# ScalarE hands the diagonal blocks of a head attention to transfers, and some vector work changes engine

## What is computed

```python
def _L0_xattn_ref(inputs, context, Wq, Wk, Wv, Wcq, Wck, Wcv, gamma, beta, W1, b1):
    ...
    a = _attention(inputs, inputs, inputs, Wq, Wk, Wv, causal=True) + inputs
    h = _layer_norm(a, gamma, beta)
    c = _attention(h, context, context, Wcq, Wck, Wcv, causal=False) + h
    h = _layer_norm(c, gamma, beta)
    f = jax.nn.relu(jnp.einsum('bse,ed->bsd', h, W1) + b1)
    out = _layer_norm(f + h, gamma, beta)
    return jax.nn.relu(out)

def _L0_attn_ref(x, W_attn, W_proj):
    ...
    att = jnp.einsum('bhqd,bhkd->bhqk', q, k) * (1.0 / math.sqrt(hd))
    causal = jnp.tril(jnp.ones((T, T), dtype=bool))
    att = jnp.where(causal, att, -jnp.inf)
    att = jax.nn.softmax(att, axis=-1)
    att = att * decay_weight_matrix(T)
    y = jnp.einsum('bhqk,bhkd->bhqd', att, v)
    y = y.transpose(0, 2, 1, 3).reshape(B, T, HEAD_QKV)
    return y @ W_proj

x = x + _L0_xattn_ref(_layernorm(x, axis=-1), ctx_1024, ...)
x = x + _L0_attn_ref(_layernorm(x, axis=-1), L0_attn_W_attn, L0_attn_W_proj)
x = x + _L0_ffn_ref(_layernorm(x, axis=-1), ...)
```

## Time and profile before

| | |
|---|---|
| median of 3 runs | 1451.5 us (1449.05 to 1451.91) |
| span of the profiled execution | 1452.8 us |
| PE busy | 1365.6 us |
| DVE busy | 1128.1 us |
| ACT busy | 601.9 us |
| POOL busy | 526.1 us |

### The profile page before, as it was taken

How to read it: one execution, slowest core, us unless ns; L and a number is a source line. 1 busy time by engine, 2 the same in 40 slices (tenths; PEclk the granted TensorE clock), 3 DMA queues, 4 the chain that set the end, 5 groups by cost and what they waited for, 6 DMA issues and landing times.

```text
span 1452.8 us, 33270 instructions
## 1 busy us (share of the span) xinstructions
PE 1365.6 (94%) x13860; PEld 851.7 (59%) x13861; DVE 1128.1 (78%) x2335; ACT 601.9 (41%) x1147; POOL 526.1 (36%) x545
## 2 busy tenths in 40 slices
PE   7679999999999999999999999999999999998888
PEld 3355566666656666665665656666665666655443
DVE  6787777777787877778778877777778877777776
ACT  2544444443444444343434444444444444443222
POOL 0133333433444333443443333343443433343222
PEclk9899999999999999999999999999999999999899
DMA  9732444433333444433333344443333344434440
GB/s 349 259 131 74 146 146 146 144 123 105 133 112 115 146 146 146 146 137 101 122 130 105 139 146 146 146 142 114 111 138 105 123 146 146 147 134 161 149 161 30
DMA packets 38662, 201.41 MB, mean 139 GB/s; under 512 B 5096, under 2 KB 5992, under 8 KB 28400
## 3 DMA queue, kind: packets, MB, share of 16 engines
q1 hardware_dynamic: 37648, 198.93, 38.3%
q10 hardware_dynamic: 864, 0.36, 0.1%
HBM read 182.24 MB, written 17.04 MB: 137 GB/s over the span
## 4 chain that ended last, share of the span: by engine, by line
PE 70%; DVE 19%; POOL 4%; ACT 4%; issue 3%; DMA 0%; DVEq 0%; POOLq 0%; ACTq 0%; SPq 0%
PE ps_a L1716 11%; PE ps_a L1739 8%; PE ps_t L1739 7%; PE ps_t L1703 6%; PE ps_a L1725 6%; PE ps_a L1751 4%; PE ps_a L1783 4%; POOL rstd L636 4%; PE ps_t L1716 3%; PE ps_v L1716 3%; DVE stats L1178 3%; DVE arena L1309 3%; PE ps_t L1826 2%; PE ps_t L1775 2%; PE ps_t L1751 2%
## 5 line engine op out<-in xcount | busy, mean ns | idle before, releaser
L645 POOL TENSOR_TENSOR act_l<-act_t,act_h 128x512 f16<-128x512 f32 (+1 forms) x176 | 199.5, 1134 | 351.4 <-ACT act_t L789 199.4
L636 POOL TENSOR_TENSOR rstd<-var,mhalf 128x1 f32<-128x1 f32 x224 | 181.8, 812 | 333.7 <-DVE var L1180 328.9
L781 ACT ACTIVATE act_h<-ps_t,scale 128x512 f16<-128x512 f32 (+1 forms) x110 | 70.8, 644 | 206.2 <-PE ps_t L1703 206.2
L645 POOL TENSOR_TENSOR last_slot<-last_slot 128x512 f16<-128x512 f32 x80 | 90.0, 1125 | 156.7 <-ACT last_slot L789 90.8
L1739 PE MATMUL ps_a<-act_h,arena 128*128 128x128 f16 x1408 | 87.6, 221 | 17.3 <-ACT act_h L781 17.3
L1739 PEld LDWEIGHTS ps_a<-act_h,arena 128*128 128x128 f16 x1408 | 81.9, 99 | 28.3 <-ACT act_h L781 21.3
L789 ACT ACTIVATE act_t<-ps_t,scale 128x512 f32<-128x512 f32 (+1 forms) x110 | 70.3, 639 | 49.1 <-PE ps_t L1703 49.1
L1739 PE MATMUL ps_t<-act_h,arena 128*128 128x128 f16 x1408 | 87.0, 221 | 3.3 <-ACT act_h L781 3.3
L1716 PE MATMUL ps_a<-arena,act_h 128*128 128x512 f16 x352 | 83.6, 380 | 1.9 <-ACT act_h L781 1.9
L1309 DVE TENSOR_SCALAR arena<-ps_a,unscale 32x512 f32<-32x512 f32 x64 | 48.2, 753 | 47.0 <-PE ps_a L1751 45.8
L1739 PEld LDWEIGHTS ps_t<-act_h,arena 128*128 128x128 f16 x1408 | 81.4, 99 | 4.9 <-DVE arena L1037 2.4
(11 more groups left out here) (380 smaller groups left out, 3150.7 us busy)
## 6 DMA issues: line engine op xcount, KB each, us to landing
arena<-in_ctx_t SPq DMA_DIRECT2D x32, 2056.0 KB, 8.4
arena<-in_ctx_n SPq DMA_DIRECT2D x32, 2048.0 KB
ctx_last<-in_ctx_last SPq DMA_DIRECT2D x32, 256.0 KB
arena<-in_ew SPq DMA_DIRECT2D x8, 1024.0 KB, 6.3
x_in<-in_x SPq DMA_DIRECT2D x22, 256.0 KB, 7.3
x_scratch<-rows SPq DMA_DIRECT2D x22, 256.0 KB, 8.8
out<-rows SPq DMA_DIRECT2D x22, 256.0 KB, 2.1
arena<-in_ew SPq DMA_DIRECT2D x8, 512.0 KB, 7.2
```

The costliest lines, as they stand in the source:

```text
L636: nc.gpsimd.tensor_tensor(rstd[s][:], var[s][:], mhalf[:], ALU.pow).then_inc(rstd_ready[s], 1)
L645: nc.gpsimd.tensor_tensor(act_l[s][:, chunks], act_t[s][:, chunks], act_h[s][:, chunks], ALU.subtract).then_inc(act_l_ready[s], 1)
L781: nc.scalar.activation(act_h[s][:, 0:width // P].rearrange("p c r -> p (c r)"), bank[s][:, 0:width], ACT.Copy, scale=scale[:, k:k + 1]).th ...
```

## The change

The block matrices get another layout, `(h c g k)` in place of `(c g h k)` for `kbd` and `(g h q)` in place of `(h g q)` for `pbd`, so that the block of a quarter of the partitions is one run of 2 KB in each partition. K is now copied from `ps_a` to `rows3` by one instruction on ACT, and the four blocks are then put in place by four transfers of 32 partitions by 512 (64 KB), a new unit "heads_k" that ACT issues. The weights are transposed by one DVE instruction of 128 by 512, and four transfers of the same size put them in place: a new unit "heads_p", issued by ACT too. The matmuls read the same numbers, now as four pieces of 32. Further: "turn_p" is a DVE transpose of the 32 by 32 blocks and no longer work of PE and ACT; POOL adds b3 to `rows3` in a new unit "x2_bias" once x2 is stored, and "ffn_out" is one instruction; the negated maximum comes out of the reduction itself, the scale XSCALE being put into `unscale`; and some waits between steps on DVE go or are made later.

```diff
-            kbd = of_arena(HALF + 5 * C * D + 16, C * G * HPC * T).rearrange("p (c g h k) -> p c g h k", c=C, g=G, h=HPC)
-            pbd = of_arena(HALF + 6 * C * D + 16, NH * G * T).rearrange("p (h g q) -> p h g q", h=NH, g=G)
+            kbd = of_arena(HALF + 5 * C * D + 16, C * G * HPC * T).rearrange("p (h c g k) -> p h c g k", c=C, g=G, h=HPC)
+            pbd = of_arena(HALF + 6 * C * D + 16, NH * G * T).rearrange("p (g h q) -> p g h q", h=NH, g=G)
...
+                def x2_bias(s, r, tile):
+                    pool.wait_ge(rows_ready[s], 6 * r + 5)
+                    pool.wait_ge(x2_stored[s], 16 * r + 32)
...
+                    nc.gpsimd.tensor_tensor(rows3[s][:], rows3[s][:], b3[:], ALU.add).then_inc(x2_biased, 1)
...
-                def turn_p(s, r, tile):
-                    act.wait_ge(p_turned[s], 2 * r + 1)
-                    nc.scalar.copy(p_t[s][:, 0:P], ps_a[s][:, 0:P]).then_inc(p_t_ready[s], 1)
...
-                def project_k(s, r, tile):
-                    act.wait_ge(k_done[s], r + 1)
+                def heads_k(s, r, tile):
+                    act.wait_ge(k_out, tile + 1)
                     if tile == 0:
                         act.wait_ge(consts_ready, 4)
                     else:
                         act.wait_ge(scored[(s - 1) % SLOTN], 3 * (r - (s == 0)) + 3)
-                    for h in (0, 1):
-                        rows = slice(HD * h, HD * (h + 1))
-                        nc.scalar.activation(kbd[rows, :, :, h, :],
-                                             ps_a[s][rows, :].rearrange("p (c g k) -> p c g k", c=C, g=G), ACT.Copy,
-                                             scale=unscale[rows, K_WATTN:K_WATTN + 1]).then_inc(k_ready[s], 1)
+                    for h in range(HPC):
+                        mine = slice(HD * h, HD * (h + 1))
+                        nc.scalar.dma_start(kbd[mine, h, :, :, :].rearrange("p c g k -> p (c g k)"), rows3[s][mine, :]
+                                     ).then_inc(k_ready, 16)
+
+                def heads_p(s, r, tile):
+                    act.wait_ge(heads_turned, tile + 1)
+                    if tile == 0:
+                        act.wait_ge(consts_ready, 5)
+                    else:
+                        act.wait_ge(y_done[(s - 1) % SLOTN], r + (s > 0))
+                    for g in range(G):
+                        mine = slice(T * g, T * (g + 1))
+                        nc.scalar.dma_start(pbd[mine, g, :, :].rearrange("p h q -> p (h q)"), rows3[s][mine, :]
+                                     ).then_inc(pbd_ready, 16)
+
+                def project_k(s, r, tile):
+                    act.wait_ge(k_done[s], r + 1)
+                    nc.scalar.activation(rows3[s][:], ps_a[s][:], ACT.Copy, scale=unscale[:, K_WATTN:K_WATTN + 1]
+                                         ).then_inc(k_out, 1)
...
-                    chain(nc.vector.reduce_max(top[s][:, 0:1], rows3[s][:, 0:P], AX.X))
-                    nc.vector.tensor_scalar(ntop[s][:], top[s][:, 0:1], -XSCALE, None, ALU.mult
-                                            ).then_inc(ntop_ready[s], 1)
+                    nc.vector.reduce_max(ntop[s][:], rows3[s][:, 0:P], AX.X, negate=True).then_inc(ntop_ready[s], 1)
+                    chain.end()
+
+                def turn_p(s, r, tile):
+                    chain = Chain("turn_p", s, r)
+                    dve.wait_ge(p_ready[s], 3 * r + 1)
+                    nc.vector.transpose(p_t[s][:, 0:P], p_n[s][:, 0:P]).then_inc(p_t_ready[s], 1)
+                    chain.last(nc.vector.reciprocal(inv[s][:, 0:1], total[s][:, 0:1]))
                     chain.end()
...
-                def project_k(s, r, tile):
-                    dve.wait_ge(k_done[s], r + 1)
...
-                    for g in range(G):
-                        rows = slice(T * g, T * (g + 1))
-                        nc.vector.transpose(pbd[rows, :, g, :], by_head(rows1[s][rows, :])).then_inc(pbd_ready[s], 1)
+                    nc.vector.transpose(sc, by_head(rows1[s][:])).then_inc(heads_turned, 1)
...
-                    chain(nc.vector.scalar_tensor_tensor(rows2[s][:], ps_a[s][:], unscale[:, K_W3:K_W3 + 1], b3[:],
-                                                         ALU.mult, ALU.add))
-                    nc.vector.tensor_tensor(rows2[s][:], rows2[s][:], rows3[s][:], ALU.add).then_inc(out_ready[s], 1)
-                    chain.end()
+                    dve.wait_ge(x2_biased, tile + 1)
+                    nc.vector.scalar_tensor_tensor(rows2[s][:], ps_a[s][:], unscale[:, K_W3:K_W3 + 1], rows3[s][:],
+                                                   ALU.mult, ALU.add).then_inc(out_ready[s], 1)
...
-                def turn_p(s, r, tile):
-                    pe.wait_ge(p_ready[s], 3 * r + 1)
-                    nc.tensor.transpose(ps_a[s][:, 0:P], p_n[s][:, 0:P], ident[:]).then_inc(p_turned[s], 1)
...
-                    pe.wait_ge(k_ready[s], 4 * r + 4)
+                    pe.wait_ge(k_ready, 64 * (tile + 1))
...
-                    pe.wait_ge(pbd_ready[s], 4 * r + 4)
+                    pe.wait_ge(pbd_ready, 64 * (tile + 1))
```

135 lines of the change are left out of this document (64 added, 71 removed), and 1 row of the table FIRST.

## The result

The changed kernel takes 1631.9 us (median of four runs, 1628.32 to 1633.86) against 1451.7 us, 1.125 times the time of the kernel before, interval 1.1227 to 1.1267. The direction was forecast, the size was not: 180 us are lost where 63 were expected, and 1631.9 lies far outside 1485 to 1560. The profiled execution spans 1626.5 us (before: 1452.8).

A forecast was written before the change was run, and what follows sets the result against it. PE's own order of work was taken as the bound, so new PE waits count fully: 1.03 + 0.82 = 1.85 us a round, 48 us over 26 rounds, plus 15 in `LAST`, 63 us in all; 1514 us predicted, range 1485 to 1560.

The forecast's parts named there:

- the landing was put at 1.7 us: Both transfer groups: 64 KB from issue to landing, estimated between an 18 KB load and 256 KB store; bounds 1.6 and 2.8.
- rival 1: Transfers land later, 2.8 us: waits of 2.0 and 1.92 us, 1575 us in all; chance 0.25 together with rivals 3 and 4.
- PE sets the pace, and a wait of PE is paid in full: Middle rounds: time saved on other engines gives nothing back; each new PE wait counts fully in 26 rounds.
- heads_k, 0.90 us late: At "head_scores": ACT's four issues start at 725.07, last block lands at 728.12, PE wants it at 727.22; 0.8 to 2.0.
- heads_p, 0.82 us late: At "head_mix": last of four issues at 739.75, landing at 741.45, against PE's start at 740.63; 0.7 to 1.9.
- Rival 1's "against": Argument against later landings: the round's context loads are not in flight at 725 to 728 nor at 740.
- x2_bias, 1.03 us, "runs beside the first wait": At "turn_xn": x2's store, POOL's addition and "ffn_out" make PE 1.03 us late, counted instead of 0.90 at "head_scores", not added.
- turn_p on DVE, a floor of 0.4 us: At "self_mix": the transpose, done at 742.1, would be 0.4 us late without the transfers; covered by the 0.82.
- Rival 3: The 128 by 512 DVE transpose takes 2.90 us: 34 us added, 1548; chance 0.25 together with rivals 1 and 4.
- its other half: Rival 3's alternative: the strided matmul read doubles the two units, 2.1 us a round, 56 us, 1570.
- First and last rounds: First rounds counted at nothing, as PE waits anyway; `LAST` at 8 for "heads_k" and 7 for "heads_p", 15 us.
- rival 4: Waits bring PE stretches at half clock: 2 us stretch costs 1 us, 26 times, 1540; chance 0.25 with rivals 1 and 3.

The follow-up runs named there:

- e1: The kernel before with "heads_k" alone: K copied whole by ACT, its four blocks sent by 64 KB transfers; 1548.2 us, ratio 1.068.
- e4: The changed kernel with the 2 MB context load held back until the K blocks have landed; 1600.7 us, ratio 1.1031.
- e11: The changed kernel with each of the eight 64 KB transfers a round cut into two of 32 KB; 2006.8 us, ratio 1.3833.
- e12: The changed kernel without "x2_bias", "ffn_out" again in two DVE instructions, both groups of transfers kept; 1620.7 us, ratio 1.1168.
- e8: The kernel before with "x2_bias" alone: POOL adds b3, "ffn_out" is one DVE instruction; 1498.5 us, ratio 1.0327.
- e7: The changed kernel with weight transfers ahead of self attention's exponential in ordinary rounds, three of four K transfers on SP, no "x2_bias"; 1513.7 us, ratio 1.0443.
- e2: The kernel before with "heads_p" alone: one 128 by 512 DVE transpose, four weight blocks sent by transfers; 1517.9 us, ratio 1.0456.

## Why the prediction was wrong

**The steps that failed.** First, the landing was put at 1.7 us for every round, and rival 1 set aside that a load might be in flight; rounds in which the last block of K meets the context load cost some 33 us (below). Second, the last rounds were costed as ordinary ones, 15 us for 47. Third, the terms of issue and landing were too small in the quiet rounds as well, 48 us for 70. The two waits themselves, at "head_scores" and "head_mix", came where they were forecast.

**PE sets the pace, and a wait of PE is paid in full.** Right: 140 us less of DVE and 26 of ACT gave no gain, and the waits found in a quiet round are, to 0.1 us, the length by which that round grew.

**heads_k, 0.90 us late.** The mechanism was right, the size was not: 1.37 us (1.42 in e1). Three terms were off. Issues behind the first take 0.61 us and not 0.45, so the last goes out 1.83 us behind the first and not 1.35 (+0.48). The landing takes 2.0 us, not 1.7 (+0.3). And the first issue does not wait for the end of "turn_pc" but starts 0.06 us after its start, 788.92 against 788.86 (-0.32). Together +0.46. The issue row I used was one that stood alone; a row with issues in line would have been needed, and none was there. **heads_p, 0.82 us late:** 1.24. The same terms, with the first issue 0.06 us behind the start of the exponential (803.87 against 803.81) and not 0.50, give 1.16. The Trainium skill, page SBUF — State Buffer, section "The DMA setup-cost knee", fits the time of a transfer by 2 us and its bytes over 436 GB/s, which gives, as an estimate, 2.15 us for 64 KB and 2.08 for 32 KB; these traces have 2.0 and 1.9, nearer to it than to the 1.7 of my line between 18 KB and 256 KB.

**Rival 1's "against", the step that failed most.** I wrote that the context loads of the round are not in flight at 725 to 728. The load of 2 MB goes out at 727.46 in that round of the kernel before, and my own last block was issued at 726.42 and landed at 728.12. As the issues really go, from 724.75 on, the fourth ends at 727.2, 0.3 us ahead of the load (in e1's regular rounds it is the same 0.3), and one late issue is enough to lose the race. e4 (the waits go when the load is held back) and e11 (they come in nearly every round when the issues end later) show the mechanism. Its price: e12's middle is 1165.5 us, of which 26 quiet rounds are 1126. Of the 39 that remain, 32.5 lie in four rounds of 48.6 to 52.6 us, with waits of 5.2 to 8.2 us and stretches at 1.2 GHz, and 6.7 in the first round of `ORDER`, which is 3.5 longer than the others in the kernel before too.

**x2_bias, 1.03 us, "runs beside the first wait".** That it hides behind "head_scores" held: 11 us by e12. Its own price was too low, 1.8 against 1.03 (e8). The step was sound at the landing it assumed and wrong in taking one landing for all, 8.7 us: the store takes 7.6 to 10.2 us in e8, and the rounds follow it. The shortest and the longest round behind the first, with the landing of the store ahead of each:

```profile
1152.72:1193.53 40.81, 39.45 (x426) 25.17 (x426) 31.34 (x67) 17.38 (x34) 17.24 (x17) 1.00 0.36 131
851.62:896.66 45.04, 41.13 (x426) 25.84 (x425) 31.34 (x67) 17.38 (x34) 17.25 (x17) 0.96 0.33 118
```

```profile
DMA to landing us min/median/max: 7.6/7.6/7.6
...
DMA to landing us min/median/max: 10.2/10.2/10.2
```

In between, a landing of 8.6 us goes with a round of 41.8 (1.2 us more than before, where I had 1.03) and one of 9.3 with 42.5: a microsecond for a microsecond. Five of the six rounds with a landing of 9.4 us or more are 1.6 us longer still, by a stretch at 1.2 GHz. The kernel before has landings of 7.7 to 10.2 us and no round that follows them.

**turn_p on DVE, a floor of 0.4 us.** Right: 0.40 in e7, where nothing else covers it. The transposes measured, in the changed kernel, 0.71 and 0.30 us:

```profile
L1359 DVE STREAM_TRANSPOSE rows<-rows x22: 711/712/714, 121.5 to 1565.0; 128x512 f32<-128x512 f32 x22
...
L1250 DVE STREAM_TRANSPOSE p_t<-p_n x32: 301/305/309, 42.6 to 1460.7; 128x128 f32<-128x128 f32 x32
```

I had said 0.7, and 0.2 with 0.35 as the bound. Rival 3 is out. So is its other half: the strided read takes 273 ns a matmul in both kernels.

**First and last rounds.** I counted 0 and 15 us; they cost 10.8 and 47. By e1 and e2 the last rounds lose 28 us to "heads_k" and 16 to "heads_p", which again add. I had costed issue and landing alone; the transfers there land among the expert loads (up to 8.9 us of wait at "head_scores"). In the first rounds it is "heads_p" (8.6 us in e2), where I let PE's old waits absorb it without having looked which unit they stood before.

**The clock**, rival 4, was right as a possibility. Quiet rounds with waits of 1.37 and 1.24 us keep 2.4 GHz. From 240 us on in `ORDER` the stretches at 1.2 GHz stand in the changed kernel behind waits of 4.0 us and more, in e8 behind 2.0 to 2.8, and in e4 behind 2.1 to 2.5 and once behind 1.35 and 1.10 us close together; a wait of 2.00 us in the changed kernel has none behind it. What it costs can be read from PE's busy time in the rounds of `ORDER`, before and in the changed kernel:

```profile
168.28:1228.23 1059.95, 1027.67 (x11068) 655.43 (x11068) 839.30 (x1751) 453.23 (x887) 415.16 (x416) 1.00 0.37 131
179.08:1354.80 1175.72, 1044.51 (x11040) 657.75 (x11040) 729.03 (x1566) 432.87 (x835) 448.89 (x443) 0.98 0.38 129
```

PE is busy for 39.50 us in a quiet round of the changed kernel, 1027.0 in 26, and 17.5 more in all. The kernel before, at full clock throughout, also has 1.7 more than 26 of its quiet rounds, so some 16 us are matmuls at half clock. They are part of the 36 and 10 us below, not a term beside them. The same working gives 10 us for e12 (1039.2 us busy), whose rounds with long waits thus lose about a third of their 32.5 to the clock.

The sum by its terms: 48 us for the middle became 70 (26 x 2.69, the quiet rounds of e12), 36 for the rounds with long waits and the first one, for which the sum had no term (those 39 less the 3.5 by which the middle before exceeds 26 quiet rounds), and 10 for what "x2_bias" adds; 15 for the last rounds became 47, and 0 for the first 11. That makes 174, the difference of the two spans.
